# Experts four steps earlier, inside the fifth superblock; scatters in eight parts without a pause; products for the row maxima spread over 14 steps

## The reference, cut to what matters

```python
xn = layernorm(x)                                  # x: [2, 2048, 128]
# attention branch
s = xn @ W_spin.T + b_spin
scores = (s @ W_J.T) @ s.T / sqrt(128)             # per batch, 2048 x 2048
local = softmax(scores) @ s
attn = tanh(beta * (s + mean(s) @ W_global.T + local))
# expert branch: 16 experts, each token uses its best 2
logits = xn @ Wg.T + bg
w, idx = top2(logits); w = softmax(w)
gate, up = split(xn @ Wgu[e] + bgu[e]); gate = min(gate, 7); up = clip(up, -7, 7)
y_e = ((up + 1) * gate * sigmoid(1.702 * gate)) @ Wd[e] + bd[e]
out = x + attn + sum over the token's 2 experts of w * y_e
```

## Time and profile before

| | us |
|---|---|
| median of 3 runs (lowest, highest) | 374.11 (373.42, 375.37) |
| profiled execution: its own time | 375.0 |
| profiled execution: span from first to last instruction | 373.2 |
| busy in the span: PE / DVE / ACT / POOL | 328.0 / 306.4 / 256.1 / 217.2 |
| scatters (first to last issue) | 100.2 to 187.4 |
| experts (first expert product to the last result landed) | 197.4 to 278.2 |
| gathers (first to last issue) | 279.0 to 363.8 |

### The profile page before, as it was taken

One profiled execution on the slowest core, in us unless ns is written; L12 is line 12 of the kernel. 1 busy time (PEld: TensorE's weight loads), 2 busy tenths in 40 slices (PEclk: granted clock), 3 DMA queues, 4 the chain that ended last, 5 costly groups with the idle time before them and its releaser, 6 DMA issues.

```text
span 373.2 us, 5903 instructions
## 1 busy us (share of the span) xinstructions
PE 328.0 (88%) x1773; PEld 272.7 (73%) x1773; DVE 306.4 (82%) x607; ACT 256.1 (69%) x509; POOL 217.2 (58%) x247
## 2 busy tenths in 40 slices
PE   2769799897999999999997999999979999997930
PEld 1547588664778788888876999999858777786720
DVE  4896877999978969969966998899798989967862
ACT  4955866674588787687683788888746776696820
POOL 5606798122577779777723345344207877777771
PEclk9997999999999999999999999999999999999985
DMA  5999600000011210212133477686453354565541
GB/s 149 327 320 365 245 4 2 0 1 30 7 50 59 75 57 26 88 49 79 57 93 91 134 235 231 203 242 207 143 171 101 98 141 128 133 142 134 124 131 56
DMA packets 41359, 45.97 MB, mean 123 GB/s; under 512 B 3770, under 2 KB 33082, under 8 KB 41330
## 3 DMA queue, kind: packets, MB, share of 16 engines
q1 hardware_dynamic: 36162, 32.94, 28.4%
q0 software_dynamic: 5168, 12.67, 12.0%
HBM read 23.46 MB, written 22.12 MB: 122 GB/s over the span
## 4 chain that ended last, share of the span: by engine, by line
POOL 37%; PE 24%; DVE 14%; issue 12%; DMA 5%; ACT 4%; SPq 1%; POOLq 0%; DVEq 0%; ACTq 0%
POOL slots_x L458 16%; POOL made L488 9%; POOL gy L488 8%; PE PS L497 4%; PE PS L499 4%; PE PS L498 4%; DVE mx L1014 4%; DMA xy<-slots_x 2%; DVE pl L999 2%; PE PS L722 2%; PE PS L604 2%; PE PS L707 2%; PE PS L551 1%; POOL rows L449 1%; PE PS L724 1%
## 5 line engine op out<-in xcount | busy, mean ns | idle before, releaser
L856 ACT ACTIVATE PS<-PS 128x512 f32<-128x512 f32 x128 | 74.8, 584 | 53.0 <-PE PS L499 51.1
L999 DVE TENSOR_TENSOR pl<-PS,ph 128x512 fp32r<-128x512 f32 x128 | 87.6, 685 | 24.8 <-ACT ph L867 24.1
L1014 DVE TENSOR_REDUCE mx<-PS 128x1 f32<-128x512 f32 x128 | 84.2, 681 | 8.7 <-PE PS L551 8.5
L867 ACT ACTIVATE ph<-PS 128x512 fp32r<-128x512 f32 x128 | 76.5, 598 | 12.4 <-ACT PS L856 0.7
L458 POOL DMA_INDIRECT slots_x<-xn,posu x64 | 62.4, 975 | 19.8 <-issue 18.9
L551 PE MATMUL PS<-xT,gq 128*128 128x512 f32 x128 | 49.1, 422 | 8.2 <-DVE mx L1014 7.8
L497 PE MATMUL PS<-ph,rows 128*128 128x512 f32 x128 | 51.6, 403 | 4.0 <-DVE pl L999 3.8
L497 PE MATMUL PS<-gq,xT 128*128 128x512 f32 x128 | 52.5, 410 | 1.3 <-DVE pl L999 1.3
L499 PE MATMUL PS<-gq,xT 128*128 128x512 f32 x128 | 50.1, 392 | 0.0
L499 PE MATMUL PS<-ph,rows 128*128 128x512 f32 x128 | 50.1, 391 | 0.0
L498 PE MATMUL PS<-pl,rows 128*128 128x512 f32 x128 | 50.0, 391 | 0.0
(11 more groups left out here) (188 smaller groups left out, 687.7 us busy)
## 6 DMA issues: line engine op xcount, KB each, us to landing
slots_y<-yr SPq DMA_DIRECT2D x20, 512.0 KB, 3.2
slots_x<-xs SPq DMA_DIRECT2D x1, 5120.0 KB, 21.8
xy<-slots_x SPq DMA_DIRECT2D x20, 256.0 KB, 3.0
xn<-in_L_attn_x SPq DMA_DIRECT2D x8, 256.0 KB, 5.2
w_f<-in_L_ffn_Wgu SPq DMA_DIRECT2D x1, 2048.0 KB, 12.9
late<-in_L_ffn_Wgu SPq DMA_DIRECT2D x1, 2048.0 KB, 18.3
xs<-in_L_attn_x SPq DMA_DIRECT2D x8, 256.0 KB, 3.3
out_y<-made SPq DMA_DIRECT2D x7, 256.0 KB, 3.1
```

Source lines behind the costliest of these rows:

```text
L856: A(S[:, n % 3], S[:, n % 3], ACT.Exp).then_inc(exp_done, 1)
L867: A(ph[:, i % RING], S[:, n % 3], ACT.Copy).then_inc(s_hi, 1)
L999: v.tensor_tensor(dst, S[:, n % 3], high.bitcast(F32), ALU.subtract).then_inc(s_lo, 1)
L1014: v.tensor_reduce(mx4[:, a, c:c + 1], MX[:, n % 2], AX.X, ALU.max).then_inc(mx_free, 1)
```

## The change

`MOE_AT` goes from 80 to 76, so the experts stand between steps 75 and 76, inside the fifth superblock (`k` = 4). Its half-finished accumulator is closed, copied by ACT to a new tile `oT_part` and later added in `fields` by four more products. One more score is placed ahead of the resumed steps. `queries(6)` moves from step 76 to 63. The 16 products and reductions for a superblock's maxima (from superblock 2 on) stand at 14 and 15 of the superblock before the one that they stood in (two of them) and at 0 to 11 (fourteen). The four subtractions between the scatters move from POOL to DVE, steps 44 to 47. The scatters' column 0 is written in four parts of 8 tiles for each half, each part waiting only for its own 8 scatters of the first half. The copy of the last group's result moves from DVE to ACT, behind `prob_hi` of step 78. The seventh block is added up within the steps (123, 124, 127), and the order of the last block's sums is turned round: first both gathers and x, then the attention's field in two halves, with `combine` behind the gathers' sums.

```diff
-    MOE_AT = 5 * TB
+    MOE_AT = 5 * TB - 4
@@ query_at
+            if i in (4 * TB - 1, 4 * TB + 12):
+                return 6 if i == 4 * TB - 1 else None
@@ maxima_at(i)
+            k, j = divmod(i, TB)
+            if j >= 14:
+                return [(k + 2, j - 14)] if k + 2 < NSB else []
+            if k + 1 >= NSB or j >= 12:
+                return []
+            if k == 0:
+                return [(1, q) for q in range(-(-4 * j // 3), -(-4 * (j + 1) // 3))]
+            first = 2 + j + (j > 4) + (j > 6)
+            return [(k + 1, q) for q in range(first, first + (2 if j in (4, 6) else 1))]
@@ GpSimd, scatters
-                    for k in range(CB, NCH):
-                        t = 4 * (k - CB)
-                        pool.wait_ge(row_h[1], k - CB + 1)
-                        g.tensor_tensor(rows[1][:, 1, t:t + 4, 1:D], xn[:, TB + t:TB + t + 4, 1:D],
-                                        rows[1][:, 0, t:t + 4, 1:D].bitcast(F32), ALU.subtract)
-                    pool.wait_ge(scat[0], 16 * NT)
-                g.tensor_copy(xn[:, :, 0], w12[:, c]).then_inc(weights_in, 1)
-                pool.wait_ge(weights_in, c + 1)
-                for t in range(NT):
+                for q in range(4):
+                    if c:
+                        pool.wait_ge(scat[0][q], 16 * NT // 4)
+                    part = slice(q * NT // 4, (q + 1) * NT // 4)
+                    g.tensor_copy(xn[:, part, 0], w12[:, c, part]).then_inc(weights_in, 1)
+                    pool.wait_ge(weights_in, 4 * c + q + 1)
+                    for t in range(part.start, part.stop):
@@ TensorE
+                if i == MOE_AT:
+                    pe.wait_ge(y_ready, 2 * NG - 3)
+                if i == 5 * TB:
+                    pe.wait_ge(y_ready, 2 * NG - 2)
-                          start=j == 0, stop=j == TB - 1)
+                          start=j == 0 or i == MOE_AT, stop=j == TB - 1 or i == MOE_AT - 1)
+                    if k == MOE_AT // TB:
+                        mm(o[:, a * w:(a + 1) * w], oT_part[:, q], AE[:, b], start=True, stop=False)
+                    pe.wait_ge(mx_free, 16 * (MOE_AT // TB + 1) + 15 + i % 2)
             down(NG - 1, 1, columns[NG - 1])
+            score(MOE_AT + 3)
@@ ScalarE, step(i)
+                if i == MOE_AT + 2:
+                    y_copy(NG - 1, 1)
@@ VectorE
+            def second_rows_lo(c):
+                t = 4 * c
+                dve.wait_ge(row_h[1], c + 1)
+                v.tensor_tensor(rows[1][:, 1, t:t + 4, 1:D], xn[:, TB + t:TB + t + 4, 1:D],
+                                rows[1][:, 0, t:t + 4, 1:D].bitcast(F32), ALU.subtract).then_inc(row_l[1], 1)
+            ROWS_AT = {44: 0, 45: 1, 46: 2, 47: 3}
+            FINISH_AT = {MOE_AT + 13 + 6 * k + 2 * (k == 6): k for k in range(7)}
-            y_copy(NG - 1, 1)
-            add_both(6)
-            add_parts(6)
-            finish(6)
+            dve.wait_ge(gat_last, 64)
+            for h in range(2):
+                dve.wait_ge(gat_half[h], 32)
+            dve.wait_ge(ld_x[7], 32)
+            m = made[:, 3]
+            link(v.tensor_tensor(m, m, gy[:, 1], ALU.add))
+            link(v.tensor_tensor(m[:, :, 0:D], m[:, :, 0:D], m[:, :, D:2 * D], ALU.add))
+            link(v.tensor_tensor(m[:, :, 0:D], m[:, :, 0:D], xs[:, 1], ALU.add))
             combine(7, 0)
             combine(7, 1)
-            dve.wait_ge(gat_last, 64)
-            ...
             for h in range(2):
                 t = slice(2 * h, 2 * h + 2)
-                dve.wait_ge(gat_half[h], 32)
-                link(v.tensor_tensor(m[:, t, 0:D], m[:, t, 0:D], gy[:, 1, t, 0:D], ALU.add))
-                v.tensor_tensor(m[:, t, 0:D], m[:, t, 0:D], gy[:, 1, t, D:2 * D], ALU.add).then_inc(fin_ready, 1)
+                dve.wait_ge(tanh_ready, NSB + h)
+                v.tensor_tensor(m[:, t, 0:D], m[:, t, 0:D], field[:, NT - 4 + 2 * h:NT - 2 + 2 * h], ALU.add).then_inc(fin_ready, 1)
```

More of the change, by code:

```diff
@@ L178, in build @@
         oh_ready, routed, eid_ready, route_done = sem("oh_ready"), sem("routed"), sem("eid_ready"), sem("route_done")
-        scat = [sem("scat0"), sem("scat1")]
+        scat = [[sem(f"scat0_{q}") for q in range(4)], [sem("scat1")]]
         weights_in, w_kept, ones_in = sem("weights_in"), sem("w_kept"), sem("ones_in")
@@ L229, in mx_no, with maxima_at @@
             return k * 17 + q
-        def maxima_at(j):
-            return range(-(-4 * j // 3), -(-4 * (j + 1) // 3)) if j < 12 else ()
+        def maxima_at(i):
+            k, j = divmod(i, TB)
[7 more added lines that the diff above has]
+            return [(k + 1, q) for q in range(first, first + (2 if j in (4, 6) else 1))]
         def rows_fill(g):
@@ L315, in _ @@
                 tokens_in(4)
-                for c in range(2):
-                    sp.wait_ge(scat[c], 16 * NT)
+                for s in scat[0]:
+                    sp.wait_ge(s, 16 * NT // 4)
+                sp.wait_ge(scat[1][0], 16 * NT)
                 sp.wait_ge(s_fill, s_no["X", CB * TB - 1] + 1)
@@ L326, in results_out @@
                 def results_out(g, u):
-                    if isinstance(g, int) and g >= NG:
-                        sp.wait_ge(y_last, 2 * (g - NG) + 2)
+                    if isinstance(g, int) and g == NG:
+                        sp.wait_ge(y_last, 2)
+                    elif isinstance(g, int) and g == NG + 1:
+                        sp.wait_ge(y_ready, 2 * NG - 2)
                     else:
@@ L647, in fields @@
             def fields(k, h):
-                o = e_bank("F", k, h)
+                if (k, h) == (7, 1):
+                    pe.wait_ge(cr_done, NSB)
+                o = MX[:, 0] if (k, h) == (7, 1) else e_bank("F", k, h)
                 b = k // CB
-                pe.wait_ge(o_kept, k + 1)
+                pe.wait_ge(o_kept, k + 1 + (k == 7 and h))
                 pe.wait_ge(e_free, e_no["M", b] + 1)
@@ L653, in fields @@
                     w, q = D + 2, slice((2 * h + a) * P, (2 * h + a + 1) * P)
-                    m = mm(o[:, a * w:(a + 1) * w], oT[:, q], AE[:, b], start=True, stop=True)
+                    if k == MOE_AT // TB:
+                        mm(o[:, a * w:(a + 1) * w], oT_part[:, q], AE[:, b], start=True, stop=False)
+                    m = mm(o[:, a * w:(a + 1) * w], oT[:, q], AE[:, b], start=k != MOE_AT // TB, stop=True)
                 m.then_inc(e_fill, 1)
@@ L658, in step @@
                 k, j = divmod(i, TB)
-                if not MOE_AT <= i < MOE_AT + 3:
+                if not MOE_AT <= i < MOE_AT + 4:
                     score(i)
@@ L664, in step @@
                     queries(query_at(i))
[L665 to L669, removed]
+                for s, q in maxima_at(i):
+                    maxima(s, q, q // 4, q % 4)
+                if k + 1 < NSB and j == 13:
+                    shift_row(k + 1)
                 if i >= LAG and not MOE_AT <= i < MOE_AT + LAG:
@@ L672, in step @@
                 if i in (MOE_AT - 2, MOE_AT - 1):
-                    if i == MOE_AT - 2:
-                        pe.wait_ge(cr_done, MOE_AT // TB + 1)
-                    turn_slots(i % 2, i % 2, i % 2 + 1)
+                    pe.wait_ge(mx_free, 16 * (MOE_AT // TB + 1) + 15 + i % 2)
+                    turn_slots(i % 2, 1 - i % 2, i % 2 + 1)
                 if i in SPIN_AT:
@@ L756, in _ @@
             gate_up(0, columns[0])
+            pe.wait_ge(t_lo, rows_fill(1) + 1)
             turn_slots(0, 0, 3)
@@ L902, in step @@
                     spins_out(*SPIN_AT[i])
-                if j == 2 and k and k != 5:
+                if j == 2 and k:
                     values_hi(k - 1)
@@ L922, in _ @@
                 step(i)
-            values_hi(4)
+            act.wait_ge(pv_done, MOE_AT)
+            A(oT_part[:], O[:, MOE_AT // TB % 2], ACT.Copy).then_inc(part_kept, 1)
             def gated_hi(n, bank, g, u):
@@ L965, in _ @@
                 step(i)
-            values_hi(7)
-            squash(7)
+            act.wait_ge(pv_done, STEPS)
+            for h in range(2):
+                A(oT[:, 256 * h:256 * h + 256], O[:, 1, 256 * h:256 * h + 256], ACT.Copy).then_inc(o_kept, 1)
+            for h in range(2):
+                act.wait_ge(e_free, e_no["F", 7, h] + 1)
+                f = field[:, NT - 4 + 2 * h:NT - 2 + 2 * h]
+                A(f, f, ACT.Tanh, scale=betac[:]).then_inc(tanh_ready, 1)
         @block.vector
@@ L1182, in finish @@
                 v.tensor_tensor(m, m, field[:, 4 * k:4 * k + 4], ALU.add).then_inc(fin_ready, 1)
+            def second_rows_lo(c):
[4 more added lines that the diff above has]
+            ROWS_AT = {44: 0, 45: 1, 46: 2, 47: 3}
             ADD_X_AT = {40: 0, 54: 1, 66: 2, 78: 3, 94: 4, 110: 5, 126: 6}
-            BOTH_AT = {MOE_AT + 11 + 6 * k: k for k in range(6)}
-            PARTS_AT = {MOE_AT + 12 + 6 * k: k for k in range(6)}
-            FINISH_AT = {MOE_AT + 13 + 6 * k: k for k in range(6)}
+            BOTH_AT = {MOE_AT + 11 + 6 * k: k for k in range(7)}
```

(10 more changed lines are left out.)

19 lines of the change are left out of this document (8 added, 11 removed).

## The result

The changed kernel took 378.38 us (median of 4, 377.7 to 379.3), the kernel before 373.76 (median of 4): ratio 1.0116, 95% interval 1.009 to 1.0142. The forecast was 381.7 (376.5 to 385.5), 7.6 us slower. A second comparison on another chip gave 377.11 against 373.55, ratio 1.0111 (1.0081 to 1.0141), so the change costs 3.6 to 4.6 us. The profiled execution took 378.62; its span is 376.9 against 373.2 before.

What follows compares the result with a forecast made beforehand. Bound by a relay of scatters, experts, last write, gathers and tail. Scatters -2.6, experts' start +0.8 and +1.6, late write +3.4, tail +4.4 sum to +7.6 on 374.1: 381.7 us, range 376.5 to 385.5.

Steps and rivals of the forecast that it cites:

- the relay: Whole kernel: time is a chain of scatters, first slots' fetch, experts, last write, gathers and short tail; attention fills in.
- Scatters: GpSimd's scatters: the pause between halves goes, -5.3, and +1.3, +0.7, +0.7 come back; end 2.6 us earlier.
- Start of the experts: TensorE from first `turn_slots` to first expert product: +0.8 for work in between, +1.6 for a low clock after waiting.
- The 20 groups: 0: Expert groups: same instructions and buffers as before, so no change in time, 0.
- The late copy: Last group's copy, now on ScalarE behind `shift_in`, `exponent` and `prob_hi`: last result written 3.4 us later.
- Gathers: GpSimd's 64 gathers: as many sums beside them as before, so 0, bounds -2 and +2 us.
- The tail: After the last gather lands: 5.3 us of sums, `combine` and tanh instead of 0.85, so +4.4 us.
- Attention ends last: Rival, last three superblocks: waits for gathers hold up `prob_lo`, adding 1 to 4 us, 383 to 386; chance 0.12.
- Collisions go: Rival, GpSimd: sums miss transfer starts, gathers -6.0 us, with scatters -7.5 in all, giving 374.2; chance 0.10.
- The clock doesn't fall: Rival, TensorE's wait at step 74: clock stays up or recovers in time, 1.6 us less, 380.1; chance 0.15.

Runs made afterwards that it cites:

- the repeats: Changed kernel and kernel before, each profiled once more without edit: changed 377.11 us, ratio 1.0111; before 373.69 us against 374.21 for the same program, ratio 0.9972.

## Why the prediction was right in direction and too high

**Right: the relay.** The stations up to the last sum came in order and within 1.2 us of the forecast (within 2.4 in the repeats). GpSimd held the experts back, TensorE stood idle for 4.42 us, its clock fell.

**Scatters, -3.0 for -2.6.** From the first to the last scatter it is -3.9 (-3.8 in the repeats) for -3.3. Between the halves the spacing is now 2.78 us with the bias transfer in it, six others are 1.44 instead of 1.26 (+1.1, forecast 1.3). Of the four subtractions one met a scatter as in the earlier trace rows (0.33 us), forecast 0.7 in all. The other +0.7, a later first scatter because of the reductions added in steps 14 and 15, is not borne out: +0.9 here, -0.2 in the repeats, and only 0.07 earlier when the maxima were put back. That it came out here is chance. (The bounds given, -4.6 and 0, are also wider than the terms give: -4.0 and -0.6.)

**Start of the experts, +2.5 for +2.4, but by luck.** In the repeats it was +1.8. The clock cost 0.7 on average instead of 1.6, and the longer way to the first product 1.45 instead of 0.8, because I left out the wait for the last maxima; the products placed in the wait separated the two. The two errors cancel in part. "The 20 groups: 0" held: from the first expert product to the end of `down(19)` it is 76.4 us in the repeat, as before, but 75.65 in this execution, a chance gain of 0.7.

**The late copy, +3.2 for +3.4.** Shown by moving it back: the 3.2 us at the copy went, and 1.6 to 3.8 us in the times.

**Gathers, 0.0 for 0:** 84.80 against 84.76. In the repeats it is 84.64 against 82.93, +1.7, so the exact hit is luck, within the bounds given.

**The tail: the step that failed.** I wrote "+4.4" and "5.5 us later all is over", as if the way from the last sum to the end were a fixed cost. The sums did grow by 4.4 us. But of the 5.5 us before, 3.2 were SyncE waiting for GpSimd's drain, a second path beside the sums. The end is the later of last sum + 2.5 and the drain; that a last sum 0.9 us earlier gained nothing while the drain was later bears this out. Measured from the last gather's start to the end, the term was +1.6 in both pairs: the drain 1.0 longer (9.24 to 10.26 from the last gather's start), and 0.6 by which the sums now reach past it. SyncE's 3.2 us at the closing line were there to be read in the trace of before; with the 3.0 of them that could be hidden taken off, the tail is 4.4 - 3.0 = +1.4, and the whole forecast would have been +4.6. That the drain itself would grow, with three more semaphores, no row of before showed.

**The rivals.** "Attention ends last" did not happen here, with 1.5 us to spare (last field product done at 367.5, gathers landed at 369.0); with the sums in the order of before it did at once. "Collisions go" had the right price (forecast 6.0, shown 5.0 with the sums taken away) and did not happen: the changed kernel has as many long gathers. "The clock doesn't fall" was worth 0.7.

**Open:** why the drain's length jumps by 1.3 us with the number of semaphores.

## What to carry to other kernels

Before a tail is priced, look at what the closing barrier waits for. A path that ends after the last result hides whatever is added to the tail up to its own end; and cutting the tail below that end gains nothing. When work is moved earlier, ask which engine releases it; here four steps bought only the 3 us by which another engine's queue had been shortened, and shortening that queue was worth nothing with the experts at their old step. A copy moved to a less busy engine is as late as what stands ahead of it in that queue.

## What the runs showed of the hardware

- After its last indirect transfer GpSimd's closing drain ends 7.91, 7.99 or 9.30 us after the end of the last issue, with 6, 13 and 16 semaphores on such transfers (3, 2 and 9 executions, each group the same to some hundredths).
- An indirect transfer's issue (0.95 us alone) that begins beside a VectorE sum of two SBUF tiles and more than 0.2 us ahead of its end, ends 0.81 to 0.85 us after the sum in 191 of 222 cases in the fourteen traces (the others take their usual time); without most of the sums 64 gathers took 5.0 us less.
- The same program against itself: ratio 0.9972 with an interval that excludes 1.
